# One GRU scan on one core: step 0 waits for half of chunk 0's tokens, and the first chunk's work is laid out anew

## The reference, cut to what matters

```python
# block 1: low-rank conditioned layer, exact gelu, ternary FFN
y = x @ W.T + fc_bias + lowrank(x, u, v) + cond
g = gelu(y)
Wq = clip(round(W / (mean(abs(W)) + 1e-5)), -1, 1)     # of W1 and of W2
x = x + relu(g @ Wq1.T + b1) @ Wq2.T + b2              # d_ff = 512
# block 2: GRU over 128 steps, then a top-1 router over 32 experts
R = sigmoid(xr + H @ Whr.T + bhr);  Z = sigmoid(xz + H @ Whz.T + bhz)
Ht = tanh(xh + (R * H) @ Whh.T + bhh)
H = Z * H + (1 - Z) * Ht;  Y = H @ Whq.T + bhq
x = x + relu(relu(Y @ w1[e] + b1[e]) @ w2[e] + b2[e])  # e = argmax of the router
```

## Time and profile before

| | us |
|---|---|
| median of three runs | 277.43 (277.11 to 277.58) |
| the profiled execution | 276.83 |
| its span, first to last instruction | 275.0 |
| outside of the span | 1.83 |
| start to the first sigmoid of step 0 | 17.43 |
| chunk 0, first sigmoid to that of chunk 1 | 33.40 |
| chunks 1 to 6 (50.83 to 234.14) | 183.31 |
| chunk 7, steps 0 to 14 | 28.84 |
| last step and the tail | 12.03 |

### The profile page before, as it was taken

One profiled execution on the slowest core, in us unless ns is written; L12 is line 12 of the kernel. 1 busy time (PEld: TensorE's weight loads), 2 busy tenths in 40 slices (PEclk: granted clock), 3 DMA queues, 4 the chain that ended last, 5 costly groups with the idle time before them and its releaser, 6 DMA issues.

```text
span 275.0 us, 8512 instructions
## 1 busy us (share of the span) xinstructions
PE 244.2 (89%) x2924; PEld 178.3 (65%) x2924; DVE 225.8 (82%) x1527; ACT 125.6 (46%) x690; POOL 17.9 (7%) x30
## 2 busy tenths in 40 slices
PE   7878987999988999899988998899988998698996
PEld 6756665667756676566755676567656666465676
DVE  2547989888898899888889889888889887878873
ACT  3243643464445544454436444554446443334432
POOL 4378000000000000000000000000000000000000
PEclk9995555556996589856995599856995599779759
DMA  7900000000000000000000000000000000000000
GB/s 255 326 6 2 4 0 4 0 2 1 2 5 19 2 4 0 21 5 0 2 23 0 2 1 4 23 0 2 4 20 2 1 2 2 20 2 0 5 21 19
DMA packets 3370, 5.61 MB, mean 20 GB/s; under 512 B 568, under 2 KB 2128, under 8 KB 3328
## 3 DMA queue, kind: packets, MB, share of 16 engines
q1 hardware_dynamic: 2992, 4.46, 4.8%
q10 hardware_dynamic: 288, 0.52, 0.6%
q0 software_dynamic: 48, 0.10, 0.1%
HBM read 4.03 MB, written 1.05 MB: 18 GB/s over the span
## 4 chain that ended last, share of the span: by engine, by line
PE 60%; DVE 26%; ACT 7%; issue 5%; DMA 1%; ACTq 0%
PE ZH L942 8%; PE R L942 6%; PE R L941 5%; DVE m_p L752 4%; DVE rh_p L718 4%; ACT R L435 4%; PE ZH L941 4%; PE O L822 3%; PE F L881 3%; ACT ZH L464 3%; PE F L804 3%; DVE rh_p L723 3%; PE F L806 2%; PE F L805 2%; DVE zh_p L727 2%
## 5 line engine op out<-in xcount | busy, mean ns | idle before, releaser
L435 ACT ACTIVATE R<-R 128x16 f32<-128x16 f32 x128 | 21.5, 168 | 74.6 <-PE R L942 73.1
L464 ACT ACTIVATE ZH<-ZH 128x16 f32<-128x16 f32 x128 | 21.5, 168 | 55.4 <-PE ZH L942 54.7
L942 PE MATMUL R<-m_p,gru_hi 128*128 128x16 f16 x254 | 45.4, 180 | 0.0
L942 PE MATMUL ZH<-rh_p,gru_hi 128*128 128x16 f16 x256 | 42.9, 181 | 1.6 <-DVE rh_p L723 0.3
L942 PE MATMUL ZH<-m_p,gru_hi 128*128 128x16 f16 x254 | 36.5, 172 | 0.0
L942 PEld LDWEIGHTS ZH<-rh_p,gru_hi 128*128 128x128 f16 x256 | 26.1, 106 | 13.2 <-DVE rh_p L723 1.0
L941 PEld LDWEIGHTS ZH<-rh_p,gru_lo 128*128 128x128 f16 x128 | 13.1, 103 | 32.1 <-DVE rh_p L718 26.3
L752 DVE TENSOR_TENSOR m_p<-keep,ZH 128x16 f16<-128x16 f32 x128 | 21.8, 170 | 12.6 <-ACT ZH L464 11.7
L941 PE MATMUL ZH<-rh_p,gru_lo 128*128 128x16 f16 x128 | 23.5, 184 | 9.5 <-DVE rh_p L718 4.1
L718 DVE TENSOR_TENSOR rh_p<-R,hist 128x16 f16<-128x16 f32 x128 | 22.3, 174 | 11.5 <-ACT R L435 4.7
L941 PE MATMUL R<-m_p,gru_lo 128*128 128x16 f16 x127 | 23.1, 182 | 5.1 <-DVE m_p L752 0.3
(11 more groups left out here) (243 smaller groups left out, 799.5 us busy)
## 6 DMA issues: line engine op xcount, KB each, us to landing
w_sb<-w SPq DMA_DIRECT2D x2, 512.0 KB, 7.5
outT<-res SPq DMA_DIRECT2D x7, 128.0 KB, 1.9
xs_sb<-xsT SPq DMA_DIRECT2D x1, 640.0 KB, 9.8
first_sb<-first SPq DMA_DIRECT2D x1, 279.0 KB, 3.7
second_sb<-second ACTq DMA_DIRECT2D x1, 256.0 KB, 3.8
ffn_sb<-ffn ACTq DMA_DIRECT2D x1, 256.0 KB, 4.7
ffn_sb<-ffn SPq DMA_DIRECT2D x1, 256.0 KB, 4.3
gru_sb<-gru SPq DMA_DIRECT2D x1, 256.0 KB, 5.3
```

The lines of the kernel that those rows point to most:

```text
L435: nc.scalar.activation(r_io, r_io, ACT.Sigmoid).then_inc(r_made, 1)
L464: nc.scalar.activation(c_io, c_io, ACT.Tanh).then_inc(cand_made, 1)
L942: return mm(out, gru_hi[:, WHR + gate, :], part, start=False, stop=low, skip_group_check=True)
```

## The change

1. **Two halves.** Chunk 0's first block, from `first_hidden` on, is computed for tokens 0 to 127 (steps 0 to 7) ahead of step 0. The other half goes into steps 0 to 2 (`first_hidden`, `first_relu`, `first_out`, `x1_first(1)`) and 3 to 6 (`project_first`, in pieces of 64 and 128 columns). The hidden layer has its own buffer with four slots, `hid_first`.
2. **Weights' scale.** `gamma` and `thresholds` run once for each weight matrix, the first as soon as W1's sum is there. DVE sums W1 ahead of its work on `first_sb`.
3. **Matmuls that nobody reads.** `keep_streaming` adds matmuls of 256 columns into PSUM columns that are not in use, 154 in all, from step 3 of chunk 0 on. It fills the places "before" and "behind" up to three, and "between" up to one, from tables for chunk 0 and by rules for the others.
4. **Chunk 0's background work**: chunk 1's first block begins in step 6, not 4; `pre_full(1)`, `pre_low_rank`, `error_function(1)`, `twice_gelu(1)`, the splits of w1 and w2 move by one to three steps, two of the w2 splits into chunk 1; `expand_off` is made on ACT in four pieces (steps 11 to 14), no longer on POOL; POOL makes `wq16` ahead of `ident`.
5. **Transfers**: `first` goes from SP's queue to ACT's and `second` from ACT's to SP's (now second there, behind W1), `gru[0:3]` to ACT's, `xs[N:3N]` ahead of `gru[3:7]`.
6. `whq` uses bank F1, not L, and its wait for `low_made` in step 15 of chunks 0 to 4 is gone.

```diff
+FIRST_LATE = 6
+KEEP_PASSES = 3
+FIRST_BEFORE = (4, 4, 2, 2, 2, 0, 2, 2, 4, 2, 2, 4, 0, 0, 3, 3)
+FIRST_BEHIND = (3, 5, 5, 2, 4, 3, 3, 2, 4, 2, 0, 2, 0, 0, 0, 3)
...
-            sp.dma_start(first_sb[:], first).then_inc(first_in, 16)
             sp.dma_start(ffn_sb[:, 0, :], ffn[:, 0, :]).then_inc(ffn1_in, 16)
+            sp.dma_start(second_sb[:], second).then_inc(second_in, 16)
...
-            act.dma_start(second_sb[:], second).then_inc(second_in, 16)
+            act.dma_start(first_sb[:], first).then_inc(first_in, 16)
             act.dma_start(ffn_sb[:, 1, :], ffn[:, 1, :]).then_inc(ffn2_in, 16)
+            act.dma_start(gru_sb[:, 0:GATES, :], gru[:, 0:GATES, :]).then_inc(gru_h_in, 16)
...
+            def first_relu(half, j):
+                act.wait_ge(first_hid_mm, NF * half + j + 1)
+                at = slice(half * 128, half * 128 + 128)
+                nc.scalar.activation(hid_first[:, j, at], F_bank[j % 2][:, at], ACT.Relu,
+                                     bias=vec[:, V_B1 + j:V_B1 + j + 1], scale=0.5).then_inc(first_relu_made, 1)
...
+            def passes_before(k, t):
+                experts, feed, last = k > 0, k < K - 1, k == K - 1
+                if k == 0:
+                    return FIRST_BEFORE[t]
+                n = 2 * (t == 0) + (t == 1) + (t == (3 if last else 5))
+                n += 2 * (feed and 2 <= t < 2 + NF) + 2 * (k < K - 2 and t in (9, 10)) + 2 * (k < K - 3 and t == 11)
+                n += 3 * (t in (LAST_HIDDEN_AT if last else HIDDEN_AT)) + 3 * (feed and t >= 14)
+                return n + 2 * (last and t == 8)
...
+            def keep_streaming(k, t, passes):
+                out = unread_bank(k, t)
+                if out is not None:
+                    for _ in range(KEEP_PASSES - passes):
+                        mm(out, gru_hi[:, WHR, :], gru_hi[:, WHZ:WHZ + 2, :], start=False, stop=False,
+                           skip_group_check=True)
...
+            def first_hidden(half, j):
+                if j >= 2 or half == 1:
+                    pe.wait_ge(first_relu_made, NF * half + j - 1)
+                pe.wait_ge(wq_made, j // 2 + 1)
+                at = slice(half * 128, half * 128 + 128)
+                mm(F_bank[j % 2][:, at], wq[:, 0, j * 128:(j + 1) * 128], g[:, at],
+                   start=True, stop=True).then_inc(first_hid_mm, 1)
...
+                    if k > 0 or t >= 3:
+                        keep_streaming(k, t, passes_before(k, t))
...
+                    if k == 0 and 3 <= t < 7:
+                        if t == 3:
+                            pe.wait_ge(x1_rest_made, 1)
+                        project_first(1 + (t - 3) // 2, 128 + (t - 3) % 2 * 64, 64)
+                    if not (experts and t in hidden_at or feed and t in (14, 15) or experts and t == 1 or step < 7):
+                        keep_streaming(k, t, KEEP_PASSES - 1)
...
-                        if k < K - 3:
-                            pe.wait_ge(low_made, 2 * k + 8)
                         whq(k, 0)
...
+                    keep_streaming(k, t, passes_behind(k, t))
```

More of the change, by code:

```diff
@@ L295, in _ @@
             pool.wait_ge(gbias_step, 2)
+            for w in range(2):
+                pool.wait_ge(wq_made, 2 * w + 2)
+                t_s(wq16[:, w, :], wq[:, w, :], 0.0, None, ALU.add).then_inc(wq16_made, 1)
+            pool.wait_ge(wq16_made, 2)
             pool.wait_ge(const_in, 16)
@@ L307, in _ @@
             pool.wait_ge(router_lo_made, 3)
-            for w in range(2):
-                pool.wait_ge(wq_made, 2 * w + 2)
-                t_s(wq16[:, w, :], wq[:, w, :], 0.0, None, ALU.add).then_inc(wq16_made, 1)
-            pool.wait_ge(expand_in, 16)
-            t_s(expand_off[0:E, :], expand_sb[:], OFF, None, ALU.mult).then_inc(expand_made, 1)
-            pool.wait_ge(expand_made, 1)
             pool.wait_ge(b1_in, 16)
@@ L450, in _ @@
                         turned_masks(k - 1)
-                    if feed and t == (10 if k == 0 else 7):
+                    if feed and t == (12 if k == 0 else 7):
                         x1_high(k + 1)
@@ L1022, in _ @@
                 low_rank(1, half)
-            first_out(0)
-            pre_full(1, start=True)
-            pre_add_bias(1)
-            first_out(1)
-            first_out(2)
-            first_out(3)
+            for j in range(NF):
+                first_out(0, j)
             pe.wait_ge(gru_x_in, 16)
             pe.wait_ge(x1_made, 1)
-            project_first(0, 0).then_inc(r_mm, 1)
-            project_first(1, 0)
-            project_first(2, 0).then_inc(z_mm, 1)
+            project_first(0, 0, 128).then_inc(r_mm, 1)
+            project_first(1, 0, 128)
+            project_first(2, 0, 128).then_inc(z_mm, 1)
             pe.wait_ge(gru_lo_made, 1)
@@ L1037, in _ @@
                 par, experts, feed, last = k % 2, k > 0, k < K - 1, k == K - 1
-                hidden_at, late = LAST_HIDDEN_AT if last else HIDDEN_AT, 4 * (k == 0)
+                hidden_at, late = LAST_HIDDEN_AT if last else HIDDEN_AT, FIRST_LATE * (k == 0)
                 if k == 1:
```

254 lines of the change are left out of this document (151 added, 103 removed).

## The result

| | before | after |
|---|---|---|
| median (lowest to highest), us | 277.27 (276.49 to 277.58), 4 runs | 269.26 (268.49 to 269.86), 4 runs |
| the profiled execution, its span | 276.83, 275.0 | 268.67, 266.8 |
| start to the first sigmoid of step 0 (term A) | 17.43 | 13.44 |
| chunk 0 (B) | 33.40 | 30.89 |
| chunks 1 to 6 (C) | 183.31 | 181.75 |

The ratio is 0.970, with a 95% interval of 0.966 to 0.974. The forecast was 269.2. The four stages of the profile give -3.99, -2.51, -1.56 and -0.15, together -8.2; the forecast had -3.5, -2.2, -2.4 and -0.15. So the sum is right to 0.1 us, but A gave 0.5 and B 0.3 more than forecast and C 0.8 less. That these cancel is luck. A second profile of the same kernel (experiment 9) has -3.81, -2.06, -1.41 and -0.31, together -7.6.

A forecast was written before the change was run, and what follows sets the result against it. It took the ring, not a busy engine, as the bound, with costs from low clock, the start and steps 0 to 2. Terms -3.5 - 2.2 - 2.4 - 0.15 = -8.25 us gave 269.2, range 266.7 to 273.0.

The forecast's parts named there:

- A: Ahead of step 0: half the first block and no wait for wq bring the first sigmoid earlier, -3.5 us.
- B: Chunk 0, 33.40 us before: shorter steps 0 to 3 and 15, steps 4 to 14 nearly unchanged, together -2.2 us.
- C: Chunks 1 to 6, 183.31 us before: clock high throughout and step 15's wait gone, 30.15 us each, -2.4 us.
- The transfers I cost at nothing: Ahead of step 0: moved loads cost nothing, as no TensorE wait there ends with a transfer; uncovered, second costs some tenths.
- What an added matmul costs: nothing: Chunks 1 to 6: at the high clock three added matmuls take 0.33 us, and expert steps carry as many at 1.88.
- D: Chunk 7 and the tail: three steps leave the low clock level, -0.15 us; the tail is untouched, at 0.
- The clock held in part: Rival: the clock may fall again in chunk 0's light beginning or lighter steps; 272.5 us, chance 0.13.
- GpSimd in the way: Rival: ahead of step 0, GpSimd work blocks VectorE once or twice, costing 1.0 to 1.5; 270.5 us, chance 0.12.
- Idle time alone: Rival: only idle time lowers the clock, so the unread matmuls change nothing; 271.2 us, chance 0.03.
- Dips that fall well: Rival: the tail runs at the high clock level and chunk 0 gains its bound of -3.0; 267.4 us, chance 0.12.
- Slower than before: Rival: at 1.2 GHz three matmuls "behind" take 0.64 and delay R's products; 284 us, chance 0.02.
- The change not doing what it says: Rival: step 0 waits for something else, such as gru_lo or W2's ternary weights; 271.2 us, chance 0.04.

The follow-up runs named there:

- experiment 9: The changed kernel run again unedited, on the chip of two further edited kernels: 268.97 us, median of six runs.
- experiment 5: The changed kernel with its transfers put back on the queues of the kernel before: 269.47 us, against 269.26 for the changed kernel.
- experiment 1: The changed kernel without its 154 unread matmuls, all else the same: 272.80 us, against 269.26 for the changed kernel.
- experiment 2: The changed kernel with one more unread matmul "before" or "between" in step 4 of chunks 1 to 6: 269.51 us, against 269.26.
- experiment 7: The changed kernel with unread matmuls only in the place "behind", none before or between: 271.28 us, against 269.26.
- experiment 12: Three gate biases moved behind the hidden layer's matmuls, against the 267.48 us kernel with more unread matmuls and other warm-ups: 267.91 us.

## Why the prediction came out

**A, -3.5 (measured -3.99): right in its steps, with one left out.** The wait for `wq` went, the queue became the next thing, and no ReLU cost more than had been allowed for. Two sizes differ in opposite ways. The start of `first_hidden`, forecast at 9.6, is 8.70 to 9.99 by the level of the clock at 4 to 10 us; the forecast took the low level and had the high one only as a bound (-4.2). That the profiled execution had the high level from the start on is luck; the second profile has -3.81. The stretch behind it takes 4.46 to 4.74 for 4.25, in after with 0.26 for `gbias`. "The transfers I cost at nothing" was wrong: with the old queues W1's sum comes 1.3 later, and `g` behind it, about 1 us for the first sigmoid in the one profile (experiment 5). It does no harm to the sum, which took PE's own queue for the last thing; that the queue is last is owed to W1's early landing.

**B, -2.2 (-2.51; -2.06 in the second profile): right in size, and in its parts as far as they were taken apart.** Steps 0 to 2 took 5.99 for a forecast of 6.15, step 3 1.96 for 2.1, steps 4 to 14 21.06 for 21.03, and step 15 1.88 for 1.95. What the forecast didn't have is how much the new layout needs the high level: without the unread matmuls it costs 32.99 (experiment 1), 1.65 to 2.10 more, where the bound for a clock that stays low up to step 7 was 1.2.

**C, -2.4 (-1.56): the mis-sized term.** Two steps failed. "With the clock high throughout, 16 x 1.88 plus 0.07": with the clock high throughout a chunk is 30.20 and not 30.15 (experiment 2), 0.3 over six chunks, as steps 2 and 4 take 1.93 each. And the clock was not high throughout: step 4 has fewer matmuls than its neighbours, three chunks fell there, and each fall cost 0.1 to 0.2, together 0.55, up to 0.17 of it from the one matmul in the place "between" of step 5. "What an added matmul costs: nothing" holds at the high level (five "behind" at 1.88). At the low one it holds for up to three of 256 columns "behind" in chunks 1 to 6, and not "between" (0.17), nor for one behind a float32 matmul in chunk 0 (0.17).

**D, -0.15 (-0.15): the same number by luck, in a stage that tells little.** Steps 3 to 5 left the low level as forecast (1.91, 1.93 and 1.92 to 1.88 each), but steps 0 to 14 give only -0.05, and another execution of the same kernel had -0.22 there; the other -0.10 is the tail, forecast at 0. The tail, "untouched", had a clock of 0.77 again in after (11.93 us), but took 10.96 to 12.72 us in the other kernels. "Where the dips fall may give or take 1 us" was about the right size.

**The rivals.** The clock held in part: partly so, at 0.55 us and not 3.3. GpSimd in the way: seen (1.65 for 0.65, by `gbias`), hidden behind PE's queue. Idle time alone: refuted by experiment 1. Dips that fall well: in neither profile of the change (tail at 0.77 both times), and true of the tail with more unread matmuls (10.98). Slower than before: refuted for the change as a whole; its mechanism is shown at the low level in step 11 of chunk 0 (experiment 7) and for six matmuls in one place (experiment 12). The change not doing what it says: refuted.
